# A three-way sum on VectorE: one strided reduce in place of two additions

## The reference

```python
radial = x[:, :N_RADIAL]
conical = x[:, N_RADIAL:N_RADIAL + N_CONICAL]
rows = jnp.concatenate([i, j])
cols = jnp.concatenate([j, i])
neighbor_sum = jax.ops.segment_sum(conical[cols], rows, num_segments=N_NODES)
deg = jax.ops.segment_sum(jnp.ones_like(rows, dtype=x.dtype), rows, num_segments=N_NODES)
deg = jnp.clip(deg, 1.0)[:, None]
agg = neighbor_sum / deg
combined = jnp.concatenate([radial, agg], axis=1)
h = jax.nn.relu(combined @ W1 + b1)
out = h @ W2 + b2
```

## Time and profile before

| | us |
|---|---|
| median of 3 runs | 4630.28 |
| range of the 3 runs | 4623.17 to 4632.92 |
| the profiled execution | 4634.52 |
| its span on the core | 4632.8 |
| third layer's stage, from its first load to the next stage's first gather | 2971.26 to 3577.61, 606.35 |
| VectorE busy in that stage | 377.78 |
| GpSimd busy in that stage | 420.79 |

### The profile page before, as it was taken

One profiled execution on the slowest core, in us unless ns is written; L12 is line 12 of the kernel. 1 busy time (PEld: TensorE's weight loads), 2 busy tenths in 40 slices (PEclk: granted clock), 3 DMA queues, 4 the chain that ended last, 5 costly groups with the idle time before them and its releaser, 6 DMA issues. The chain is left out here.

```text
span 4632.8 us, 31253 instructions
## 1 busy us (share of the span) xinstructions
PE 2329.6 (50%) x8870; PEld 1410.8 (30%) x8870; DVE 2920.4 (63%) x3922; ACT 956.6 (21%) x1485; POOL 3413.1 (74%) x3151
## 2 busy tenths in 40 slices
PE   7820067775787830000622331177675567767763
PEld 3410044443455520000622331022222334434432
DVE  8876177775888856666211110166665799999995
ACT  0012022221455521111000000144443111111110
POOL 7777677774777747775688888777773777777776
PEclk9965555555899965555655555588887777777776
DMA  1034244442444432222122222344443111111110
GB/s 29 12 104 157 51 95 99 99 99 61 149 157 153 161 108 66 66 82 58 4 5 5 5 5 5 56 144 151 151 147 99 30 33 28 26 33 28 27 32 9
DMA packets 348974, 327.86 MB, mean 71 GB/s; under 512 B 223275, under 2 KB 295862, under 8 KB 347596
## 3 DMA queue, kind: packets, MB, share of 16 engines
q1 hardware_dynamic: 85600, 236.67, 14.2%
q0 software_dynamic: 144256, 45.62, 10.4%
q10 hardware_dynamic: 118944, 43.56, 3.9%
HBM read 170.38 MB, written 156.58 MB: 71 GB/s over the span
## 5 line engine op out<-in xcount | busy, mean ns | idle before, releaser
L1399 POOL DMA_INDIRECT sum_table<-e_add_rows,e_add_idx x392 | 613.3, 1565 | 142.9 <-issue 117.7
L1943 PE MATMUL g_pX<-w,g_h_T 128*128 128x512 f32 x784 | 444.6, 719 | 157.6 <-DVEq L1797 157.5
L536 POOL DMA_INDIRECT g_ring<-x_table,pos x392 | 390.2, 995 | 176.7 <-issue 119.2
L536 POOL DMA_INDIRECT f_ring<-con_table,pos x392 | 420.8, 1073 | 134.3 <-issue 127.3
L536 POOL DMA_INDIRECT c_ring<-x_table,pos x392 | 387.9, 989 | 169.0 <-issue 124.3
L536 POOL DMA_INDIRECT b_ring<-h_table,src x392 | 406.0, 1036 | 132.8 <-issue 125.9
L1761 POOL DMA_INDIRECT out_x<-g_out_rows,end_index x392 | 413.9, 1056 | 121.2 <-issue 119.2
L536 POOL DMA_INDIRECT d_ring<-g_table,pos x392 | 378.5, 966 | 167.8 <-issue 124.1
L345 POOL DMA_INDIRECT x_dst<-in_x,dst x392 | 398.9, 1018 | 130.5 <-issue 130.5
L1669 PE MATMUL f_pH<-f_T,w2in 128*128 128x448 f32 x672 | 318.0, 619 | 276.2 <-DVE f_T L1561 276.2
L1450 PE MATMUL e_pS<-e_values,e_equal 128*128 128x18 f32 x784 | 169.1, 378 | 380.0 <-DVEq L1424 380.0
(11 more groups left out here) (346 smaller groups left out, 5198.0 us busy)
## 6 DMA issues: line engine op xcount, KB each, us to landing
f_sums<-sum_table ACTq DMA_DIRECT2D x126, 238.0 KB
sum_table<-c_zero SPq DMA_DIRECT2D x39, 715.0 KB
g_table<-c_g SPq DMA_DIRECT2D x42, 448.0 KB, 2.5
h_table<-a_xp SPq DMA_DIRECT2D x28, 560.0 KB, 3.3
a_x<-in_x SPq DMA_DIRECT2D x28, 448.0 KB, 5.8
b_h_node<-h_table ACTq DMA_DIRECT2D x28, 448.0 KB, 4.3
b_x_node<-in_x SPq DMA_DIRECT2D x28, 448.0 KB, 4.8
x_table<-b_x_node SPq DMA_DIRECT2D x28, 448.0 KB, 2.5
```

What stands on the lines that cost most here:

```text
L536: pool.indirect_dma_start(out=ring[:, t, :], out_offset=None, in_=table, in_offset=bass.IndirectOffsetOnAxis(ap=idx[:, c * C + t:c * C + t ...
L1399: pool.indirect_dma_start(out=g.sums[b], out_offset=bass.IndirectOffsetOnAxis(ap=aidx[:, c % 2, t:t + 1], axis=0), in_=add[:, c % 2, t, :] ...
L1943: last = nc.tensor.matmul(pX[d % 2][:, j * 512:(j + 1) * 512], tsb[:, 0, quad], g.w3[:, (2 * d + j) % 4, :], start=True, stop=True)
```

## The change

In `first`, the loop of two additions (each followed by a drain) is replaced by one `tensor_reduce` over the table axis. Its input is all three tables' parts, read with the table axis innermost: three numbers 1904 bytes apart, then the next row's three. Its output is a new tile `total` of 128 x 28 x 17, one buffer for all jobs, where before the sum was left in table 0's part of `sums`. All later instructions of `first` read `total`. No other instruction is added, removed or moved, and no semaphore changes: on every engine the order is as before, with one reduce where the two additions stood.

```diff
+        total = sb("total", [P, C, CW])
...
             def first(j):
                 (kind, k), b = jobs[j], j % 2
                 dve.wait_ge(here[b], 16 * R * (j // 2 + 1))
-                total = sums[:, b, 0]
-                for i in range(1, R):
-                    nc.vector.tensor_tensor(total, total, sums[:, b, i], ALU.add)
-                    dve.drain()
+                nc.vector.tensor_reduce(flat(total), sums[:, b].rearrange("p r t w -> p (t w) r"), AX.X, ALU.add)
+                dve.drain()
```

## The result

The changed kernel is slower: 4648.13 us median of 5 runs (4645.3 to 4651.87) against 4631.74 us for 5 runs of the kernel before (4623.17 to 4632.92), a ratio of 1.004 with an interval of 1.0026 to 1.0053. The direction was forecast, and the time lies inside the range, but the loss is 16 us where the forecast had 38.

The account below looks back on a forecast made before the run. The prediction took VectorE's work plus a DMA round trip it sets off as the bound. It added 34.0 us for the reduce and 4 for the clock, 38.0 together: 4668 us median, range 4637 to 4686.

Parts of the forecast that it names:

- the rival with the free stride: In the new reduce, distance costs nothing: 1.63 us each, a 7.3 us term, 4638 us in all; chance 0.12.
- The forecast's own range: Range for the kernel's time without the free stride: 4650 to 4686 us.
- the sign by which it would be wrong: In the new profile, a reduce under 2 us would show the forecast wrong.
- The path: In the third layer's stage, 27 of 42 sums lengthen VectorE's rounds one for one; 15 are hidden by waits.
- The price of the reduce: In VectorE's sums, 2.62 us per reduce against 1.38 or 1.34 for two additions: 34.0 us longer.
- the lower end of 1.63: Bound from below for the new reduce, if distance costs nothing: 1428 x 1.042 + 145 = 1.63 us.
- The clock term: TensorE's restarts on each round's third f_T slow after longer pauses: 4 us, between 0 and 8.3.
- The rival with the gathers: GpSimd's gathers set the pace and no longer stretch behind the sums: 14.0 us off, 4616 us; chance 0.03.
- The rival of the instruction count: In VectorE's sums, one reduce costs what one addition costs: 27 x 0.7 us off, 4611 us; chance 0.02.

Follow-up runs that it names:

- the 27 sums: Changed kernel with the reduce only for the 27 sums held to be on VectorE's path, additions for the other 15: 1.0041 against the kernel before.
- the 15: Changed kernel with the reduce only for the 15 sums held to be hidden by waits, additions for the rest: 1.0006 against the kernel before.
- the edge job's: Kernel before, edge job's additions moved: before the third job's radial wait, 1.0002; in another run to the head of its round, 0.9968 (4616.87 us).
- the order that does pay: Changed kernel with the reduce reading order number, row, so triples also lie far apart: reduce 2.80 us, kernel 4682.17 us in one run.
- The last two runs: Kernel before with late fill(c-1), edge sum at its round's head, ACT's mask copy behind the last output: 4612.43 us with additions, 4597.75 us with the reduce.

## Why the prediction was right, and where it was off

**The number.** 4648.13 us lies in the whole range of 4637 to 4686 only because its lower end was taken from the rival with the free stride. The forecast's own range began at 4650, and the sign by which it would be wrong, a reduce under 2 us, came true. So the direction was right by the path; that the time fell inside the range is owed to the rival and not to the forecast.

**The path** was right: the 27 sums as a group count and the 15 show no cost, the third of each round is covered by the radial wait (still 13 times, 8.4 us each), and the gathers are awaited only in round 0. Of the single sums in the two groups none was tried alone but the edge job's.

**The price of the reduce** is the step that failed: "Steps of 64, 112 and 128 bytes cost about the same, so I take 1904 bytes at that price". The step was taken as the property that counts. In the rows that it came from, two things go together: numbers that lie far apart, and no early return to the neighbourhood of one just read. The new reduce has only the first. L849 comes back beside a number it has read after 16 reads and L1584 after 28, and both pay; the reduce comes back after three. Where between three and 16 the price sets in was not tried. The reduce takes 1.78 us, 0.15 above the lower end of 1.63 and far below 2.62, so the term was 27 x 0.41 = 11 us and not 34. The rival with a free stride named the reason ("Each line is read again after three reads") and gave it 0.12. Its term, 7.3 us, is short by those 0.15 us a sum, which make it 11; the 16 us that were measured are more than either, by what was left open above. The lower end itself was exact: 1.62 us with neighbouring addends.

The Trainium skill (Advanced Engine Details and Errata, SBUF Cachelines) wants at least two hits on a 16-byte line in succession. Read to the letter, all 1428 reads of the changed kernel would pay, since each goes to another line than the last. The runs differ: 1.78 us, where the order that does pay takes 2.80. The measurement decides, and a return to the line three reads later avoids most of the price.

**The clock term** failed too. Four us were added for slower restarts of TensorE, and none of it shows. Of the restarts on the third `f_T` that the timelines show with a pause, 7 of 12 took more than 1.77 us in the kernel before and 6 of 13 in the changed one, although the mean pause grew from 1.9 to 2.4 us. The waits for f_out_T fell from 48.6 to 43.8 us; that fall is not the longer sums', for it is there too (44.8) where the reduce is off the path. The timeline of TensorE in the changed kernel shows four of these restarts, to set beside the earlier trace rows:

```profile
3127.39 1.77 PE L1668 MATMUL f_pH<-f_T,w2in 128*128 128x448 f32 x4 [2.68 <-DVE f_T L1560]
...
3251.26 2.76 PE L1668 MATMUL f_pH<-f_T,w2in 128*128 128x448 f32 x4 [2.68 <-DVE f_T L1560]
...
3417.51 1.77 PE L1668 MATMUL f_pH<-f_T,w2in 128*128 128x448 f32 x4 [2.31 <-DVE f_T L1560]
...
3500.91 3.23 PE L1668 MATMUL f_pH<-f_T,w2in 128*128 128x448 f32 x4 [2.81 <-DVE f_T L1560]
```

After pauses of 2.31 and 2.68 us the four multiplications still took 1.77 us, where the kernel before took 2.32 after 2.01; and after another pause of 2.68 us in the changed kernel they took 2.76. The windows around two of these restarts, and around the one of the kernel before at 3161.44:

```profile
3126.00:3132.00 6.00, 4.61 (x18) 1.92 (x19) 4.31 (x5) 2.92 (x5) 3.72 (x3) 1.00 0.60 194
3500.00:3506.00 6.00, 5.09 (x15) 1.74 (x15) 3.06 (x3) 1.98 (x3) 4.47 (x6) 0.72 0.63 202
...
3160.00:3166.00 6.00, 4.56 (x13) 1.38 (x14) 3.51 (x4) 1.89 (x4) 4.62 (x5) 0.72 0.61 177
```

The granted clock was 1.00 (2.4 GHz) around the restart at 3127.39, and 0.72, between 2.4 and 1.2 GHz, around the other two. The length of the pause alone does not tell whether the clock holds; I had read a rule out of four rows. What else decides was not tried.

**The rival with the gathers** was wrong about the pace of this kernel, but right in its mechanism and its size. By my count of the timelines the gathers lost 14.0 us behind the additions and lose none behind the reduce. The last two runs show what that is worth where the gathers are the pace. The Trainium skill (GPSIMD Engine Reference, Key points) says that GpSimd shares its SBUF interfaces with VectorE, and that it contends there with VectorE instructions that have two SBUF inputs; 1.40 us against 0.95 agrees. The rival of the instruction count has nothing for it: one instruction took 0.41 us more than two.

## What to carry to other kernels

Price a strided read by the order in which lines are visited, not by the step alone: if the next outputs read beside the last ones, a far step between addends is nearly free (0.15 us of 1.78 here), and a loop order that jumps at every read costs 1.70 to 1.86 ns a number in place of 1.04. Two short additions still beat one reduce over the same data: at about 1.04 ns a number the reduce passes 1428 numbers where the additions pass 952, and even with neighbouring addends it took 1.62 us against 1.38. And before judging such an edit, ask which engine is the pace: the reduce lost 16 us where VectorE was, and won 15 where the gathers were, because they no longer run long behind it.

## What was not expected of the hardware

A single reduce shape took 1.62, 1.78 or 2.80 us by the order of its reads alone. And TensorE kept a granted clock of 1.00 around a pause of 2.68 us in one kernel, where it had a mean of 0.72 around a pause of 2.01 us in the other.
